# A fused four-layer kernel: attention's output projected beside the last scores, and the first rounds of the scan stage reordered

## The reference, cut

```python
xn = _layernorm(x)
x = x + mamba_forward(xn') + mamba_backward(xn')      # two directions, 256 channels, 16 states each
      + ffn(xn)                                        # xn is its x
# in ffn:
o = softmax(q @ k.T / sqrt(8)) @ v                     # 16 heads of 8, over each layer-normed row
x2 = xn + (o @ wo + bo)
hn2 = layernorm(x2) * ln2_g + ln2_b
idx = argmax(hn2 @ gate_w + gate_b)                    # one of 8 experts for each token
out = x2 + (relu(hn2 @ w1[idx] + b1[idx]) @ w2[idx] + b2[idx])
# in mamba, for each channel and state:
h = exp(dt_t * A) * h + (dt_t * u_t) * B_t;   y_t = sum(h * C_t)
```

## Time and profile before

| | us |
|---|---|
| median of 3 runs (1328.2 to 1328.93) | 1328.55 |
| the profiled execution | 1332.02 |
| its span | 1330.3 |
| DVE busy | 1196.1 (90%) |
| PE busy | 1036.7 (78%) |
| ACT busy | 892.0 (67%) |
| POOL busy | 503.1 (38%) |

### The profile page before, as it was taken

The page is one execution under the profiler, slowest core; times in us unless marked ns, Lnnn a source line. Parts: engine busy times, 40 slices in busy tenths (PEclk is TensorE's granted clock), DMA queues, the critical chain, the costliest instruction groups (busy, mean ns, idle before and its releaser), DMA issues. The chain is left out here.

```text
span 1330.3 us, 18174 instructions
## 1 busy us (share of the span) xinstructions
PE 1036.7 (78%) x6017; PEld 340.5 (26%) x6017; DVE 1196.1 (90%) x1754; ACT 892.0 (67%) x1352; POOL 503.1 (38%) x359
## 2 busy tenths in 40 slices
PE   2789996888888888888888888857564887978753
PEld 1443321111111111111111111123211344444211
DVE  8892667999999999999999999756999999999997
ACT  6444558777777777777777878858255666767531
POOL 5030113300000000000001221258699999899994
PEclk9989997999999999999999999975656788787665
DMA  3034333200000033000001100053336867774521
GB/s 100 0 130 150 135 127 119 83 1 1 1 29 15 15 64 64 29 20 11 17 17 33 33 4 15 2 129 79 66 85 143 223 147 172 168 186 108 117 69 34
DMA packets 78831, 97.77 MB, mean 73 GB/s; under 512 B 12259, under 2 KB 42778, under 8 KB 78738
## 3 DMA queue, kind: packets, MB, share of 16 engines
q1 hardware_dynamic: 77714, 94.51, 27.3%
q0 software_dynamic: 1024, 2.10, 0.5%
HBM read 70.73 MB, written 25.56 MB: 72 GB/s over the span
## 5 line engine op out<-in xcount | busy, mean ns | idle before, releaser
L886 DVE TENSOR_REDUCE at_mpart<-psum 128x1 f32<-128x512 f32 x1024 | 637.6, 684 | 41.6 <-PE psum L1067 38.5
L858 ACT ACTIVATE at_probs<-psum 128x1024 f32<-128x1024 f32 x512 | 495.4, 1022 | 141.3 <-PE psum L1097 140.5
L1471 POOL TENSOR_TENSOR t_inject<-shared 128x1024 f32<-128x1024 f32 x120 | 281.2, 2352 | 55.8 <-POOLq L60 19.3
L1067 PE MATMUL psum<-at_ks,at_qs 56*128 56x512 bf16 x1024 | 202.5, 392 | 100.2 <-DVE at_mpart L886 99.5
L1110 PE MATMUL psum<-at_probs,at_vg 128*32 128x512 f32 x2048 | 273.7, 606 | 0.7 <-ACT at_probs L858 0.6
L715 POOL CAST at_m<-at_mneg 128x16 bf16<-128x16 f32 x16 | 4.0, 251 | 546.5 <-DVE at_mneg L891 540.9
L1543 ACT ACTIVATE psum<-shared,aneg 128x512 f32<-128x512 f32 x240 | 164.9, 692 | 54.6 <-DVE t_hc L1672 43.8
L1740 DVE TENSOR_TENSOR_SCAN psum<-psum,last,t_inject 128x512 f32<-128x512 f32 x146 | 181.0, 1276 | 4.4 <-ACT psum L1543 4.1
L1869 PE MATMUL psum<-t_hc,stack 128*32 128x512 f32 x480 | 95.4, 878 | 96.9 <-DVE t_hc L1672 55.7
L1097 PE MATMUL psum<-at_qs,at_ks 59*128 59x512 bf16 x1024 | 157.2, 379 | 7.5 <-ACT at_probs L858 6.2
L1067 PEld LDWEIGHTS psum<-at_ks,at_qs 56*128 56x128 bf16 x1024 | 49.3, 93 | 422.9 <-DVE at_mpart L886 408.7
(11 more groups left out here) (258 smaller groups left out, 1054.9 us busy)
## 6 DMA issues: line engine op xcount, KB each, us to landing
shared<-mp_dt_d SPq DMA_DIRECT2D x64, 256.0 KB, 5.4
shared<-mp_dtu_d SPq DMA_DIRECT2D x64, 256.0 KB, 8.9
t_w<-in_w SPq DMA_DIRECT2D x46, 256.0 KB
mp_u_d<-shared SPq DMA_DIRECT2D x8, 512.0 KB, 4.6
mp_z_d<-shared SPq DMA_DIRECT2D x8, 512.0 KB, 4.4
mp_dt_d<-shared SPq DMA_DIRECT2D x8, 512.0 KB, 2.8
mp_dtu_d<-shared SPq DMA_DIRECT2D x8, 512.0 KB, 2.7
shared<-mp_u_d SPq DMA_DIRECT2D x16, 256.0 KB, 3.8
```

Of the source, the lines that this page charges most:

```text
L858: act.activation(probs[:, u_ % 2, p, :], s_pair[p], ACT.Exp, scale=float(HD) ** -0.5).then_inc(probs_ready, 1)
L886: dve.reduce_max(mpart[:, s % 2, 2 * jp + b, i, kc:kc + 1], ring[x % 3], AX.X).then_inc(ring_free, 1)
L1067: pe.matmul(ring[z_ % 3], qs[half(b, DQ), buf, of_pair(jp, c * CH + i * P, P)], ks[half(b, DQ), buf, of_pair(jp, kc * CH, CH)], start=True ...
L1471: pool.tensor_tensor(inject[:, k % NI:k % NI + 2, :], dus[:, i % 2, j:j + 2, :], bs[:, m % NBC, :].unsqueeze(1).to_broadcast([P, 2, CH]), ...
```

## The change

Front: in the last units PE turns the attention's output of chunks 0 to 2 (`early_turn`, behind units 238, 243 and 247), ACT copies it (`early_copy`, units 239, 244, 248), PE multiplies it by wo (`early_project`, units 240, 245, 249), and DVE adds it to `S.xn1` and takes its statistics (`early_added`, units 241, 246, 251). They use the one ring bank that is free then. Only chunk 3 stays in the tail.

Tail: the first inject is cut into its two tiles. In rounds 4 to 11 DVE weighs its two tiles right behind their second scan. Ln and Exp come at tile 6, `shifts` at tile 7, `variances` at tile 2; standardising is at tiles 10 to 13, with two of each chunk's four tiles of tokens on POOL. DVE's logits go to tiles 22, 23, 25 and 26, `choose` to 27, the placing to 31 to 33. At the end, the first part of the last projection (two matmuls that add gathered rows) is issued ahead of the last sums, and the add of gathered chunk 3 is made in round 62 instead of round 63.

```diff
+        x2_bank = ring[(rows_at[NSTEP - 1] - 1) % 3]
+        TURN_AT, COPY_AT, PROJECT_AT, ADD_AT = (3, 8, 12), (4, 9, 13), (5, 10, 14), (6, 11, 16)
...
+            def early_copy(c):
+                act.wait_ge(e_turned, c + 1)
+                if c:
+                    act.wait_ge(e_projected, c)
+                act.activation(S.oT, x2_bank, ACT.Copy).then_inc(e_copied, 1)
...
+                if u_ - U0 in COPY_AT:
+                    early_copy(COPY_AT.index(u_ - U0))
...
+            def early_added(c):
+                dve.wait_ge(e_projected, c + 1)
+                x2 = S.xn1[:, TPC * c:TPC * (c + 1), :]
+                dve.tensor_tensor(x2, x2, x2_bank.rearrange("p (i d) -> p i d", d=P), ALU.add).then_inc(e_added, 1)
+                dve.wait_ge(e_added, c + 1)
+                for i in range(TPC * c, TPC * (c + 1)):
+                    dve.bn_stats(S.st6[:, i, :], S.xn1[:, i, :])
...
+            def early_turn(c):
+                pe.wait_ge(ring_free, turned_at[NSTEP - NCH + c])
+                if c:
+                    pe.wait_ge(e_added, c)
+                else:
+                    pe.wait_ge(ring_free, rows_at[NSTEP - 1])
+                for i in range(TPC):
+                    mm = pe.transpose(x2_bank[:, P * i:P * (i + 1)], S.v_all[:, P * (TPC * c + i):P * (TPC * c + i + 1)], S.ident[:, :])
+                mm.then_inc(e_turned, 1)
+
+            def early_project(c):
+                pe.wait_ge(late_in, 16 * 7)
+                pe.wait_ge(consts, LAST_CONST - 1)
+                pe.wait_ge(e_copied, c + 1)
+                for i in range(TPC):
+                    mm = pe.matmul(x2_bank[:, P * i:P * (i + 1)], S.oT[:, P * i:P * (i + 1)], S.wo[:, :], start=True, stop=True)
+                mm.then_inc(e_projected, 1)
...
+                if u_ - U0 in PROJECT_AT:
+                    early_project(PROJECT_AT.index(u_ - U0))
+                if u_ - U0 in TURN_AT:
+                    early_turn(TURN_AT.index(u_ - U0))
                 if u_ - U0 in (7, 11, 14, 17):
                     early_sums((7, 11, 14, 17).index(u_ - U0))
...
+            def standardize(c):
+                pool.wait_ge(shift_ready, 1)
+                for i in range(TPC * c + 2, TPC * (c + 1)):
+                    pool.tensor_scalar(xn[:, i, :], S.xn1[:, i, :], rstd[:, i:i + 1], shift[:, i:i + 1], ALU.mult, ALU.add)\
+                        .then_inc(xn_pool, 1)
...
-                    pool.tensor_tensor(inject[:, k % NI:k % NI + 2, :], dus[:, i % 2, j:j + 2, :],
-                                       bs[:, m % NBC, :].unsqueeze(1).to_broadcast([P, 2, CH]), ALU.mult).then_inc(injected, 2)
+                    for l, w in (((j, 1), (j + 1, 1)) if k == K0 else ((j, 2),)):
+                        pool.tensor_tensor(inject[:, l:l + w, :], dus[:, i % 2, l:l + w, :],
+                                           bs[:, m % NBC, :].unsqueeze(1).to_broadcast([P, w, CH]), ALU.mult).then_inc(injected, w)
                 weigh(k - NI + 1)
+                if K0 + 10 <= k < K0 + 10 + NCH:
+                    standardize(k - K0 - 10)
...
-                for i in range(TPC * c, TPC * (c + 1)):
+                for i in range(TPC * c, TPC * c + 2):
                     act.activation(xn[:, i, :], S.xn1[:, i, :], ACT.Identity, bias=shift[:, i:i + 1], scale=rstd[:, i:i + 1])\
...
-                if K0 + 12 <= k < K0 + 12 + NCH:
-                    standardize(k - K0 - 12)
-                if k == K0 + 8:
+                if K0 + 10 <= k < K0 + 10 + NCH:
+                    standardize(k - K0 - 10)
+                if k == K0 + 6:
                     act.wait_ge(var_ready, 1)
...
-                weigh(k - 1)
+                if r >= SCATTER:
+                    weigh(k - 1)
+                if r < SCATTER:
+                    weigh(k)
...
-                if K0 + 1 <= k < K0 + 1 + NCH:
-                    attention_sums(k - K0 - 1)
-                if k == K0 + 4:
+                if k == K0 + 1:
+                    attention_sums(NCH - 1)
+                if k == K0 + 2:
                     variances()
-                if k == K0 + 9:
+                if k == K0 + 7:
                     shifts()
...
-                if k in (K0 + 21, K0 + 24):
-                    logits(0 if k == K0 + 21 else 2)
-                    logits(1 if k == K0 + 21 else 3)
-                if k == K0 + 25:
+                if k - K0 in (22, 23, 25, 26):
+                    logits((22, 23, 25, 26).index(k - K0))
+                if k == K0 + 27:
                     choose()
-                if K0 + 29 <= k < K0 + 32:
-                    place[k - K0 - 29]()
+                if K0 + 31 <= k < K0 + 34:
+                    place[k - K0 - 31]()
...
-                    if r in (GATHER + 5, GATHER + 7):
-                        experts_out(2 + (r - GATHER - 5) // 2)
+                    if r in (GATHER + 5, GATHER + 6):
+                        experts_out(2 + r - GATHER - 5)
...
-            for c in range(NCH):
+            for c in (NCH - 1,):
                 for i in range(TPC):
                     mm = pe.transpose(S.banks[4 + c][:, P * i:P * (i + 1)], S.v_all[:, P * (TPC * c + i):P * (TPC * c + i + 1)], S.ident[:, :])
                 mm.then_inc(o_turned, 1)
...
+                if r == NR - 1:
+                    last_out = begin_out(NN - 1)
                 sums(r)
...
-            project_out(NN - 1)
+            project_out(NN - 1, *last_out)
```

More of the change, by code:

```diff
@@ L511, in front_stage @@
         e_weighed, e_summed, e_gated = sem("e_weighed"), sem("e_summed"), sem("e_gated")
+        e_turned, e_copied, e_projected, e_added = sem("e_turned"), sem("e_copied"), sem("e_projected"), sem("e_added")
         block = ctx.enter_context(nc.Block())
@@ L999, in _ @@
                     maxima(n)
+                if u_ - U0 in ADD_AT:
+                    early_added(ADD_AT.index(u_ - U0))
                 if u_ == U0:
@@ L1557, in attended @@
             def attended(c):
-                act.wait_ge(o_turned, c + 1)
+                act.wait_ge(o_turned, 1)
                 act.activation(oT[:, cols(c)], S.banks[4 + c], ACT.Copy).then_inc(oT_ready, 1)
@@ L1565, in _ @@
                 if k == K0:
-                    for c in range(NCH):
-                        attended(c)
+                    attended(NCH - 1)
                 if m == 0:
@@ L1704, in attention_sums @@
                 x2 = S.xn1[:, TPC * c:TPC * (c + 1), :]
-                dve.wait_ge(o_done, c + 1)
+                dve.wait_ge(o_done, 1)
                 add_to(x2, S.banks[4 + c].rearrange("p (i d) -> p i d", d=P)).then_inc(o_added, 1)
-                dve.wait_ge(o_added, c + 1)
+                dve.wait_ge(o_added, 1)
                 for i in range(TPC * c, TPC * (c + 1)):
                     ins = dve.bn_stats(st6[:, i, :], S.xn1[:, i, :])
-                if c == NCH - 1:
-                    link(ins)
+                link(ins)
             def variances():
@@ L1775, in take @@
                 if x < R:
-                    pe.wait_ge(o_added, NCH)
+                    pe.wait_ge(o_added, 1)
                 else:
@@ L1792, in turn_normed @@
                 out = take("N", c)
-                pe.wait_ge(xn_ready, TPC * (c + 1))
+                pe.wait_ge(xn_ready, 2 * (c + 1))
+                pe.wait_ge(xn_pool, (TPC - 2) * (c + 1))
                 for i in range(TPC):
@@ L1833, in result, with begin_out @@
                 mm.then_inc(side_full, 1)
-            def project_out(n):
+            def begin_out(n):
                 out = take("O", n)
@@ L1843, in project_out @@
                               start=True, stop=False)
+                return out, more
+            def project_out(n, out, more):
                 pe.wait_ge(y_free, NB * (n + 1) - 1)
@@ L1876, in _ @@
                 mm.then_inc(o_turned, 1)
-            for c in range(NCH):
-                pe.wait_ge(oT_ready, c + 1)
+            for c in (NCH - 1,):
+                pe.wait_ge(oT_ready, 1)
                 for i in range(TPC):
@@ L1887, in _ @@
                 if (n := chunk_at(r, 10)) is not None:
-                    project_out(n)
+                    project_out(n, *begin_out(n))
                 if (s := slot_at(r, 1)) is not None:
@@ L1926, in build @@
         S.shared = sb(ctx, "shared", [P, 32 * CH])
-        S.gated0 = S.shared[:, 30 * CH:31 * CH]
+        S.gated0, S.oT = S.shared[:, 30 * CH:31 * CH], S.shared[:, 31 * CH:32 * CH]
+        S.st6 = sb(ctx, "st6", [P, NT, 6])
         S.last = sb(ctx, "last", [P, NB * NQ * NJ])
```

4 lines of the change are left out of this document (2 added, 2 removed).

## The result

The changed kernel took 1334.68 us (median of 7; 1334.24 to 1339.2) against 1329.8 of the kernel before (median of 7; 1328.2 to 1330.7): ratio 1.0047, 95% interval 1.0036 to 1.0057. By the ratio it is slower by 6.2 us (the medians lie 4.9 apart), and outside the range of 1323.5 to 1332.0. Its profiled execution took 1334.59 (span 1332.9), against 1332.02 (span 1330.3) before. Three of its seven executions took 1338.06 to 1339.2 and four 1334.24 to 1334.68; the profiled one is of the four, and no trace shows what parts the two groups.

A forecast was written before the change was run, and what follows sets the result against it. It took VectorE as full through most of the page, with ScalarE's exps pacing the last scores and PE's chain the first tail rounds. Terms +3.3 - 4.5 - 1.0 + 2.0 = -0.2 us gave 1328.3 as median; range 1323.5 to 1332.0.

The forecast's parts named there:

- The front: Last attention units: early projection of three chunks delays ScalarE's exps, +3.3 us (bounds 1.4 to 6.3).
- Rival D: Front hides nothing: 6.3 us, total 1331.3; with a tail of -1.5 as well 1334.3; chance 0.07.
- The tail's chain: Tail rounds 6 to 10: PE's sums, spreads and turns bind; round 6's sums at 33.4, tile 18's scan at 42.6.
- Rival C: Tail: standardise operations on GpSimd are slower; at 1.66 us each +8.4, total 1336.7; chance 0.09.
- and the placing, whose length I keep: Tail behind choose: placing keeps its length, 17.9 us less 3.5 now ahead, so the old 84.2 state comes at about 79.7.
- the term -4.5 for the tail: Tail's first rounds: the new order wins 4.5 us (bounds -1.5 to -11.6), going through undiminished from round 12.
- the rule: Moved add: VectorE operation with two SBUF inputs and GpSimd operation reading SBUF exclude each other for a whole instruction; loses 2.0.
- Rival E: Tail: later rounds take back freed time, waiting on ScalarE or the logits; tail -1.5, total 1331.3; chance 0.08.
- A: Tail: PE doesn't bind rounds 6 to 10, GpSimd's queue does; -11.6 instead of -4.5, 1321.3; chance 0.20 including part.
- The moved add: Round 62: gathered chunk 3's add clashes with GpSimd's inject, 2.6 us lost, 0.6 won: +2.0 (bounds 0 and 2.2).
- Rival B: End: no clash at the moved add, total 1326.3; chance 0.12.
- the step "-1.0": End: two matmuls move ahead of the last sums into PE idle, so the last projection starts earlier: -1.0 us.

The follow-up runs named there:

- mended changed kernel: Changed kernel with small operations in PSUM, casts on GpSimd, ends' scan relieved, both adds behind the last weighing, tiles 1024 bytes further: 1321.23 us, ratio 0.9935.
- the two mended versions of the kernel before: Kernel before with choice and ends' scan relieved, both gathered adds behind the last weighing: 1324.96 us (0.9956) with last projection's matmuls moved, 1325.33 (0.9961) without.

## Why the prediction was wrong, point by point

**The front: right.** +3.3 predicted, 3.1 measured, with the gaps where they were said to be. Rival D is out as far as the front goes.

**The tail's chain: its figures met up to the scan of tile 18, in part by luck.** Round 6's sums start at 33.7 (33.4 predicted; the terms as printed add up to 32.85, and without rounding to 33.3), tile 18's scan at 42.7 (42.6). Two errors cancel in that: a standardise operation on GpSimd is 0.44 us long (438 to 453 ns, eight of them), not 0.61, which saves 1.4 us in all, and the shift took 4.73. With the shift and the variances relieved, tile 18's scan stands at 41.0. Rival C is out by this length, and the first of the eight, 0.14 us behind the weighing before it, paid nothing extra.

**The failed step: "and the placing, whose length I keep", and with it every small VectorE operation that was costed by its row of before.** Tile 22's scan starts at 51.4 instead of 50.2 (the cast's 2.35 had delayed tile 15's scan, its inject, weighing and the sums of round 7, 42.4 instead of 41.1). The choice starts 0.9 late, at 62.4, and takes 4.8 instead of 3.7: its end stands at 67.2, not 65.2. The placing is 0.7 longer: full 1.78 for 0.74, passed 3.01 for 1.66, ends 0.80 for 1.88, the clamp of expert numbers 0.18 for 0.74. 2.0 + 0.7 is the 2.7 by which 4.5 was too much. So the term -4.5 for the tail measured -1.8 in this trace and -2.4 to -2.8 in the three others of the same tail code. The lengths of before were no lengths of these operations. The pick's 2.45 and the ends' 1.88 in the kernel before were waits for GpSimd too (0.30 and 0.17 with an input in PSUM), of the phase that it happened to have. I had the rule in hand for one add at the end and did not hold it against the operations of rounds 4 to 12, which the change puts beside a GpSimd that is 93% busy instead of 81% (900 to 925).

The Trainium skill, "SBUF — State Buffer", Who interferes with whom, lists copy, cast and tensor_scalar among the VectorE operations that can hold the shared port pair, beside those with two SBUF inputs, and says that tensor_reduce never does on trn2. The traces agree: the cast took 2.35, the one-input tensor_scalar of the variances 1.63, and no reduction of choice or placing over 0.37.

**Rival E, by another road.** It held that the tail's gain would be lost, -1.5, but to ScalarE and the logits; the gain was 1.8, and the loser was VectorE, by waiting for GpSimd. A did not come: PE's clock was 0.50 from 885 to 925.

**The moved add: right.** 2.69 long (2.6 predicted); the run that undoes it gives 2.3 back, the traces have 1.7, and +2.0 was forecast. Rival B is out.

**The end: right about where, wrong about what.** The gap of 0.80 is there, and the matmuls lie under it. But the step "-1.0" kept the projection's 2.3 us, which it has only if PE comes to it without a pause; behind the 0.80 it took 3.68. The term of 1.0 is nothing by the traces. What the profile wins behind the scan of tile 236 is not its doing: 17.5 us in the changed kernel, 17.3 in the version with the matmuls moved back, 18.6 in the kernel before, which has an add more there (and 18.5 in another trace of the changed tail, so it is not steady either). The wake-up of 0.2 was 0.06 here.

**A term that was missing: +1 to 2 us for the place of the tiles.** Clear of zero it is only in the kernel before. Nothing in the diff's order of work shows it, only the moved allocation.

**The sum as the runs have it**, in us against the kernel before: front with its gain in the tail and the tiles' place +2.8, moved add +2.3, moved matmuls 0; the 1.1 that is left of 6.2 is the rest of the tail's order, within the intervals nothing. Predicted for the same: +3.3 - 4.5 + 2.0 - 1.0. Up to round 13 the mended changed kernel is 3.5 to 6.0 us ahead of the four versions of the kernel before with a relieved choice, which is what -4.5 would look like without the waits.

**What stays open.** The three high executions of the changed kernel lie 3.4 to 4.5 us over its median, and no trace is of one; the ratio, which takes them in, has a loss of 6.2 where the medians have 4.9. How much of the missing gain by round 13 each single operation took can't be told apart, since a wait that is removed can turn up at a later operation. And from round 13's first scan to round 54's it took 273.2 to 277.8 us over all traces. Of the two mended versions of the kernel before, whose work is the same there, one loses 1.8 us in round 24, where the clock rises later. PE's four spreads in the one and in the other:

```profile
1042.45 3.78 PE L1792 MATMUL psum<-t_bc_rows,t_sel 32*128 32x512 f32 x4
```
```profile
1040.61 2.30 PE L1792 MATMUL psum<-t_bc_rows,t_sel 32*128 32x512 f32 x4
```

Why the rise comes where it comes was not tried.

## What to carry to other kernels

Where GpSimd works without pause, cost no VectorE operation by its row: ask whether it has two inputs in SBUF or is a copy, cast or tensor_scalar from SBUF to SBUF, and price it at up to the rest of GpSimd's back-to-back operations. One input or the output in PSUM takes the wait away, but part of the wait can move on to the next such operation that is left as it was. And an add with both inputs in SBUF belongs where GpSimd is done; a matmul moved ahead to fill a gap can cost the engine the clock of what follows.

## What the hardware showed that I had not expected

- VectorE waits not only for the GpSimd operation that is running: the shift of 0.15 us waited 4.73, through the rest of an inject, a second inject and a weighing, though GpSimd's queue passed from one to the next twice. In other executions it came in at such a seam after 1.15. The Trainium skill, "SBUF — State Buffer", SBUF: two separate sides, has the one that comes first hold the ports for its whole instruction; which of the two is next at a seam no run here settles.
- GpSimd's inject of 128x1024 depends on where its tiles lie: medians of 2351 to 2354 ns at one place, 2372 to 2410 when they are moved by 384 bytes, 2351 and 2352 when by 1024.
- The last projection of 16 matmuls takes 3.56 to 3.78 us behind 0.80 us of idle, at a mean granted clock of 0.50 to 0.55 (1.2 GHz nearly throughout), and 1.95 to 3.12 behind sums and matmuls without a gap, at 0.61 to 1.00, since the clock rises to 2.4 GHz ahead of it or within it.
- A two-scalar tensor_scalar of 128x128 on GpSimd takes 0.44 us, less than the 0.61 of the one-scalar form in the earlier trace rows.
